# Decoder kernel on one core: the last stage regrouped into quads of heads on row and column tiles

## The reference, cut

```python
x = x + _L1_attn_ref(_layernorm(x), w_qkv, w_out, b_out)        # 16 heads of 32, key blocks of 128
x = x + _L1_xattn_ref(_layernorm(x), ctx, ctx, Wq, Wk, Wv, Wfc, bfc)  # 32 heads of 16, 8 key groups
x = x + _L1_ffn_ref(_layernorm(x), ...)   # base matmul + rank-16 adapters, gates top 2 of 6
# attention with blocks j of 128 keys:
m_ij = jnp.max(s, axis=-1, keepdims=True)
p = jnp.exp(s - m_ij)
l_ij = jnp.sum(p, axis=-1, keepdims=True)
m_new = jnp.maximum(m, m_ij)
alpha = jnp.exp(m - m_new)
beta = jnp.exp(m_ij - m_new)
l_new = alpha * l + beta * l_ij
out_new = alpha * l / l_new * out + beta * l_ij / l_new * pv
```

## Time and profile before

| | us |
|---|---|
| median of three runs | 3021.64 |
| lowest and highest | 2979.6, 3046.27 |
| profiled execution | 3025.3 |
| its span, first to last instruction | 3024.0 |
| PE busy | 2710.3 (90%) |
| DVE, ACT, POOL busy | 1141.2, 696.0, 569.6 |
| mean granted PE clock | 0.889 |

### The profile page before, as it was taken

One profiled execution on the slowest core, in us unless ns is written; L12 is line 12 of the kernel. 1 busy time (PEld: TensorE's weight loads), 2 busy tenths in 40 slices (PEclk: granted clock), 3 DMA queues, 4 the chain that ended last, 5 costly groups with the idle time before them and its releaser, 6 DMA issues.

```text
span 3024.0 us, 30202 instructions
## 1 busy us (share of the span) xinstructions
PE 2710.3 (90%) x10527; PEld 1605.8 (53%) x10527; DVE 1141.2 (38%) x2956; ACT 696.0 (23%) x2195; POOL 569.6 (19%) x1202
## 2 busy tenths in 40 slices
PE   7999999888699956999779999999998999999978
PEld 4555555555466633555446546464554645546544
DVE  2333433399522220111134534434354342534432
ACT  1111111000011101111133423424233251433412
POOL 0010110255100041111022221222112121221200
PEclk9777997699899987999969898988989899798979
DMA  4111110011222215222312002020020302103030
GB/s 150 35 35 35 63 35 21 25 42 44 106 80 87 80 35 174 63 63 63 99 58 44 23 10 56 15 58 22 22 44 15 58 22 44 37 1 59 1 58 8
DMA packets 93622, 150.62 MB, mean 50 GB/s; under 512 B 15472, under 2 KB 46960, under 8 KB 93344
## 3 DMA queue, kind: packets, MB, share of 16 engines
q1 hardware_dynamic: 86768, 130.05, 15.3%
q0 software_dynamic: 6704, 18.64, 2.2%
HBM read 106.33 MB, written 41.80 MB: 49 GB/s over the span
## 4 chain that ended last, share of the span: by engine, by line
PE 37%; issue 6%; DVE 3%; ACT 2%; POOL 2%; DMA 0%; DVEq 0%; SPq 0%; POOLq 0%; ACTq 0%
PE psum L1220 10%; PE psum L1341 8%; PE psum L1253 5%; PE psum L1309 3%; PE psum L1273 2%; PE psum L1262 2%; PE psum L1382 2%; PE psum L1330 2%; ACT probA L1435 1%; POOL yg L1679 1%; DVE xn L335 1%; DVE m_col L1629 1%; DVE statA L1580 1%; PE psum L346 1%; PE psum L1394 1%
## 5 line engine op out<-in xcount | busy, mean ns | idle before, releaser
L1341 PE MATMUL psum<-ex,va 128*32 128x256 f32 x1024 | 292.8, 415 | 24.4 <-ACT oe L1478 24.1
L1629 DVE TENSOR_REDUCE m_col<-psum 128x2 f32<-128x512 f32 x256 | 172.8, 686 | 123.6 <-PE psum L1309 123.6
L1435 ACT ACTIVATE probA<-psum,statA 128x128 f32<-128x128 f32 x512 | 180.8, 368 | 151.4 <-DVE statA L1580 151.4
L1472 ACT ACTIVATE ex<-psum 128x512 f32<-128x512 f32 x256 | 153.2, 602 | 197.1 <-PE psum L1330 194.5
L647 PE MATMUL psum<-kv,toep 128*128 128x288 f32 x640 | 165.2, 415 | 36.7 <-DVE z L663 32.4
L1047 PE MATMUL psum<-wgu,xgT 128*128 x624 | 190.2, 461 | 0.0
L442 PE MATMUL psum<-w,xnT 128*128 128x512 f32 x384 | 169.2, 598 | 6.8 <-DMA w<-in_wq 6.8
L1253 PE MATMUL psum<-kT,qT 32*128 32x256 f32 x512 | 169.0, 459 | 2.7 <-ACT statA L1439 2.7
L1341 PEld LDWEIGHTS psum<-ex,va 128*32 128x32 f32 x1024 | 97.1, 115 | 126.1 <-ACT oe L1478 28.9
L647 PEld LDWEIGHTS psum<-kv,toep 128*128 128x128 f32 x640 | 121.0, 193 | 80.7 <-issue 44.7
L1309 PE MATMUL psum<-k_stack,q_stack 48*128 48x256 f32 x512 | 144.4, 383 | 17.1 <-issue 13.4
(11 more groups left out here) (231 smaller groups left out, 4443.9 us busy)
## 6 DMA issues: line engine op xcount, KB each, us to landing
q_stack<-q_parts_d SPq DMA_DIRECT2D x48, 256.0 KB, 6.4
wgu<-in_exp_gate_up SPq DMA_DIRECT2D x8, 1408.0 KB, 7.5
ys_d<-ys SPq DMA_DIRECT2D x39, 256.0 KB
toep<-kpad_d SPq DMA_DIRECT2D x32, 256.0 KB, 3.0
q_parts_d<-q_part SPq DMA_DIRECT2D x32, 256.0 KB, 3.5
xin<-in_x SPq DMA_DIRECT2D x8, 512.0 KB, 5.7
cin<-in_ctx SPq DMA_DIRECT2D x8, 512.0 KB, 6.0
ctxT_d<-ctxT SPq DMA_DIRECT2D x8, 512.0 KB, 3.3
```

The costliest lines, as they stand in the source:

```text
L1341: i = pe.matmul(out_x[quad:quad + DA, 0:S], va[:, kt, h // 4, :], ex[n % 4][:, kt, :], start=kt == 0, stop=kt == TT - 1, skip_group_check= ...
L1435: act.activation(p[:, t, j * P:(j + 1) * P], src[:, (TT * t + j) * P:(TT * t + j + 1) * P], ACT.Exp, bias=s3[:, 0, TT * t + j:TT * t + j + 1],
L1472: act.activation(ex[n % 4][:, :, :].rearrange("p t s -> p (t s)"), ring_x.at[step, n], ACT.Exp).then_inc(s("x_exp"), 1)
L1629: dve.tensor_reduce(m_col[tile % 2][:, :, h % HPT], ring_x.at[step, n].rearrange("p (t k) -> p t k", t=TT), AX, ALU.max, negate=True).then ...
```

## The change

Heads go in quads. In self-attention a quad is one block m: four heads on the four groups of 32 partitions. `a_max` computes the scores of a quad with queries on the partitions (eight matmuls, four row tiles, four PSUM banks) only for the block maxima (two reduces of 1024 elements on DVE). `a_stat` makes the weights of the blocks, `a_rows` turns maxima and weights into rows, writes them to DRAM and reads them back: a row of negated maxima for each head (`mrow`) and the weights spread over 32 partitions each (`ab`). `a_exp` computes the scores again, transposed, and adds the maxima with a matmul of one contraction row; ACT takes the exponential in two pieces of 1024. `a_values` sums over the keys with a matmul against ones and multiplies with the values, both on four column tiles, and five DVE operations weight, add and divide. No transposes of probabilities, no scaling and no work on POOL are left there.

In cross-attention four key groups i stand 32 partitions apart (`q_spread`, `k_spread`), a quad is one query head c of each group. fp32r and the split into parts are gone: plain fp32 with 16 rows (17 with the maximum). `x_max`, `x_exp` and `x_values` work on quads (8 of each for a batch).

All eight banks are one ring for both threads (`Ring`), with takes of one bank or of an even pair. Of the order: x_k and x_v stand ahead of norm ln5, `base` stands behind `lowT`, norms, xb5 and xb6 have changed places, the routed rows are gathered in two halves through one buffer, and the totals of `together` are the threads' own sums.

```diff
+    def take(self, key, sem, n, wide=1):
+        k = self.n % self.size
+        if wide == 2 and k % 2:
+            k = (k + 1) % self.size
+        self.n = k + wide
+        before = self.freed[k:k + wide]
+        self.freed[k:k + wide] = [(sem, n)] * wide
+        self.at[key] = k
+        return k, before
...
+        return ([(0, 6000, "routed", b), (0, 1200, "routed_add", b, 0), (0, 6000, "routed_more", b),
+                 (0, 1200, "routed_add", b, 1)] + norm_steps("ln4", b) + [(0, 0, "xb4", b)] + turn_steps("x4", b))
...
+    def self_attention(b):
         out = []
...
+        for m in range(KD):
+            out += [(1710, 0, "a_qk", b, m, n) for n in range(2)] + [(860, 0, "a_max", b, m)]
+        out += [(0, 0, "a_stat", b)] + [(3430, 0, "a_v", b, t) for t in range(TT)] + [(220, 6500, "a_rows", b)]
+        quads = [("a_exp", 0), ("a_exp", 1), ("a_values", 0), ("a_exp", 2), ("a_values", 1), ("a_exp", 3), ("a_values", 2),
+                 ("a_values", 3)]
+        quads = [(1710, 0, step, b, m) for step, m in quads]
+        quads[-2:] = [quads[-2][:1] + (1500,) + quads[-2][2:], quads[-1][:1] + (3500,) + quads[-1][2:]]
+        out += side_by_side(quads, routed_in(b + 1) if b < B - 1 else [], 0)
+        return out + [(3430, 0, "a_out", b, t) for t in range(TT)]
...
+        quad = lambda step, a, c, wait=0: (860, wait, step, b, a, c)
+        out = [quad("x_max", 0, c) for c in range(4)] + [quad("x_max", 1, 0), (220, 0, "x_rows", b, 0)]
+        out += [quad("x_max", 1, c) for c in range(1, 4)]
+        out += [quad("x_exp", 0, 0), (220, 0, "x_rows", b, 1), quad("x_exp", 0, 1)]
+        every = [(a, c) for a in range(2) for c in range(4)]
+        for n in range(2, 8):
+            out += [quad("x_values", *every[n - 2]), quad("x_exp", *every[n])]
+            if n == 6:
+                out.append((880, 0, "x_divide", b, 0))
+        out += [quad("x_values", *every[6], 1000), (440, 0, "x_back", b, 0), quad("x_values", *every[7], 800)]
+        return out + [(880, 1800, "x_divide", b, 1), (440, 900, "x_back", b, 1)]
...
+        out = [(0, 0, "x_in", b), (1710, 0, "x_k", b), (1730, 0, "x_v", b)] + norm_steps("ln5", b) + [(0, 0, "xb5", b)]
+        out += turn_steps("x5", b)
+        out += [(1710, 4500 if m == KD - 1 else 0, "x_q", b, m) for m in range(KD)]
+        out += heads(b) + [(3430, 800 * t, "x_out", b, t) for t in range(TT)]
+        out += norm_steps("ln6", b) + [(0, 0, "xb6", b)] + turn_steps("x6", b)
+        out += [(820, 0, "low", b, t) for t in range(TT)]
+        out += [(0, 250, "gate", b, n) for n in range(3)] + [(0, 600, "gate", b, 3)]
+        out += [(0, 250, "gate", b, n) for n in range(4, 12)] + [(0, 600, "gated", b)]
+        return out + [(220, 0, "lowT", b)] + [(4290, 0, "base", b, t) for t in range(TT)] + [(0, 0, "out", b)]
 
...
+    ahead, behind = alone(self_attention(0)), alone(cross(0))
     for b in range(B - 1):
-        order += together((cross(b), 1.01 * ahead), (self_attention(b + 1), ahead))
+        order += together((cross(b), behind), (self_attention(b + 1), ahead))
...
+                    elif step == "a_rows":
+                        b, = a
+                        on_sp.wait_ge(s("a_row"), b + 1)
+                        on_sp.wait_ge(s("d_ab"), 80 * b)
+                        sp.dma_start(rows_d, mrows[:, :]).then_inc(s("d_rows"), 16)
+                        on_sp.wait_ge(s("d_rows"), 16 * (b + 1))
+                        on_sp.wait_ge(s("a_second"), KD * b)
+                        on_sp.wait_ge(s("a_w"), KD * b)
+                        by_head = rows_d.rearrange("(w m r j) s -> w r m j s", w=2, m=KD, r=HG)
+                        sp.dma_start(mrow[0:P:DA, :, :, :], by_head[0]).then_inc(s("d_ab"), 16)
+                        for r in range(HG):
+                            sp.dma_start(ab[DA * r:DA * r + DA, :, :], bass.AP(
+                                rows_d.tensor, (2 * HA + TT * r) * S, [[0, DA], [HG * TT * S, KD], [1, TT * S]])).then_inc(
+                                    s("d_ab"), 16)
...
+                    elif step == "a_max":
+                        b, m = a
+                        on_pe.wait_ge(s("qk1"), 8 * b + 2 * m + 2)
+                        two = [pe_take((step, b, m, p), s("a_m"), 8 * b + 2 * m + p + 1, 2) for p in range(2)]
                         for t in range(TT):
...
+                            for r in range(HG):
+                                c = slice(DA * r, DA * r + DA)
+                                i = pe.matmul(bank[two[r // 2] + r % 2][:, t * S:(t + 1) * S], qT1[c, m, part(t)], kT1[c, m, :],
+                                              start=True, stop=True)
...
+                        two = [pe_take((step, b, m, p), s("a_exp"), 8 * b + 2 * m + p + 1, 2) for p in range(2)]
                         for kt in range(TT):
...
+                            for r in range(HG):
+                                c = slice(DA * r, DA * r + DA)
+                                pe.matmul(bank[two[r // 2] + r % 2][:, kt * S:(kt + 1) * S], kT1[c, m, part(kt)], qT1[c, m, :],
+                                          start=True, stop=False)
...
+                        l = pe_take(("a_l", b, m), s("a_w"), n + 1)
+                        for j in range(TT):
+                            for r in range(HG):
+                                pe.matmul(bank[l][DA * r:DA * r + DA, j * S:(j + 1) * S], ones[:, 0:DA], e[:, r, j * S:(j + 1) * S],
+                                          start=True, stop=True, skip_group_check=True)
...
+                            for i in range(4):
+                                r = slice(DA * i, DA * i + DX)
+                                ins = pe.matmul(bank[two[i // 2] + i % 2][:, t * S:(t + 1) * S], q_spread[r, slot, part(t)],
+                                                k_spread[r, half, :], start=True, stop=True)
...
+                                r = slice(DA * i, DA * i + DX + 1)
+                                ins = pe.matmul(bank[two[i // 2] + i % 2][:, kt * S:(kt + 1) * S], k_spread[r, half, part(kt)],
+                                                q_spread[r, slot, :], start=True, stop=True)
...
+                            for i in range(4):
+                                ins = pe.matmul(bank[k][DA * i:DA * i + DA, 0:S], va[:, kt, 4 * half + i, :],
+                                                e[:, i, kt * S:(kt + 1) * S], start=kt == 0, stop=kt == TT - 1, skip_group_check=True)
...
+                        for p in range(2):
+                            k = ring.at[step, b, m, p]
+                            act.activation(e[:, 2 * p:2 * p + 2, :], psum[:, k:k + 2, :], ACT.Exp).then_inc(s("a_exp"), 1)
...
+                    elif step == "a_max":
+                        b, m = a
+                        on_dve.wait_ge(s("a_rT"), b)
+                        on_dve.wait_ge(s("a_first"), KD * b + m + 1)
+                        for p in range(2):
+                            k = ring.at[step, b, m, p]
+                            dve.tensor_reduce(mc[:, :, 0, m, 2 * p:2 * p + 2, :].rearrange("p t r j -> p r t j"),
+                                              psum[:, k:k + 2, :].rearrange("p r (t j k) -> p r t j k", t=TT, j=TT), AX, ALU.max,
+                                              negate=True).then_inc(s("a_m"), 1)
...
+                        b, m = a
+                        n = KD * b + m
+                        on_dve.wait_ge(s("d_ab"), 80 * (b + 1))
+                        on_dve.wait_ge(s("a_o"), n)
+                        on_dve.wait_ge(s("a_values"), n + 1)
+                        dve.tensor_tensor(wx[:, 0, :], bank[ring.at["a_l", b, m]], ab[:, m, :], ALU.mult).then_inc(s("a_w"), 1)
+                        on_dve.wait_ge(s("a_w"), n + 1)
+                        dve.tensor_tensor(wx[:, 1, :], bank[ring.at[step, b, m]], wx[:, 0, :], ALU.mult).then_inc(s("a_x"), 1)
+                        on_dve.wait_ge(s("a_x"), n + 1)
+                        dve.tensor_tensor(ds, wx[:, :, 0:S], wx[:, :, S:2 * S], ALU.add).then_inc(s("a_ds"), 1)
+                        on_dve.wait_ge(s("a_ds"), n + 1)
+                        dve.reciprocal(ds[:, 0, :], ds[:, 0, :]).then_inc(s("a_rc"), 1)
+                        on_dve.wait_ge(s("a_rc"), n + 1)
+                        on_dve.wait_ge(s("a_out"), 2 * b)
+                        dve.tensor_tensor(oT1[:, m, :], ds[:, 1, :], ds[:, 0, :], ALU.mult).then_inc(s("a_o"), 1)
...
+                        out = bank[pe_take((step, b, t), s("x6r"), 2 * b + t + 1)]
+                        for k in range(KD):
+                            pe.matmul(out, xT2[:, k, part(t)], load["w_base"][:, k, :], start=k == 0, stop=False)
                         on_pe.wait_ge(s("lowT"), b + 1)
```

633 lines of the change are left out of this document (258 added, 375 removed).

## The result

The changed kernel takes 2876.93 us (median of four runs, 2857.87 to 2883.43) against 3017.39 us on the same chip (four runs, 2979.6 to 3046.27): a ratio of 0.956, 95% interval 0.946 to 0.967. The forecast was 2833 us, range 2730 to 2950. Direction and size are right; the result lies 44 us above the point.

The account below looks back on a forecast made before the run. PE was taken to set the end. Work 103, waits 50 and clock 7 gave a period of 160 us against 178.6; saving 130, tail 44 and prologue 14 from 3024 gave 2836, as median 2833 us, range 2730 to 2950.

Parts of the forecast that it names:

- PE slots: PE work per period at full clock: 90.8 us removed, 42 added as quads, 61 unchanged; from 152 to 103, saving 49.
- The places of the waits: Where PE idles per period, including cT's load 2.7 us, a_exp for rows 4, turn of x6 11, gates 8.
- The reciprocal at its upper bound: DVE in a_values: reciprocal of 256 elements bounded by 0.42 and 1.78 us, the upper taken; 4.3 us a quad.
- The idle sum: PE's waits over one period, walked in the new order: 50 us in all, the largest 13 in x_max.
- The clock term: Per period: four idles, each followed by about 4 us of work at half clock, cost some 7 us.
- Tail: Cross part of the last batch alone: 105 us with half clock against 149 before, saving 44.
- with half clock 105: End of the tail's walk: 99 us, raised to 105 for work at half clock.
- rival 2: Clock stays at half over narrow work; over 3400 us with all 80 us on the path; chance 0.05 for slower.
- half clock over x_exp to x_out: A listed sign that the prediction is wrong: PE at half clock from x_exp through x_out.
- 1: Rival: only two tiles overlap, quads cost 1.73 us, period 186, total about 3040 us; chance 0.10.
- 3: Rival: waits are less than summed, period falls to 135 us, total about 2660; chance 0.08.
- 4: Rival: an unseen wait chain adds 10 us a period, 2906 total; slower only from +27, chance 0.02 for that.

Follow-up runs that it names:

- e8: Changed kernel with six unused full-width projections added in the tail only, one behind each of x_values 0 to 5 of the last batch; 2861.5 us (before 2988.42).
- e1: Changed kernel with all four matmuls of every score quad on one row tile, computing one head four times; 3865.88 us (before 3024.34).

## Why the prediction was right, and where its terms were off

- **PE slots: right.** 103 us of work after, 152 before, saved 49. Measured at the full clock in the steady periods: 108.5 and 152.9, saved 44. Counted by line (each record's own time multiplied by the granted clock), the quads come to 44.1 us against my 42 and the rest to 64.4 against my 61, so most of the 5.5 us is in the projections and turns, which I had taken from counts alone. The quads of x_exp cost 1.07 us and not 0.96; those of a_values 0.87.
- **The places of the waits: right but for one.** cT 2.2 (predicted 2.7), a_exp for the rows' DMA 6.7 (4, with bounds of 2 and 6, so just outside), the turn of x6 behind two a_values 10.1 (11), three short waits in a_max 1.4 for the 2.25 counted. In the place of the gates (8) PE waits 3.4, and in a steady period it is ln4's normalization that ends the wait. The reciprocal at its upper bound was right, 1.75 for 1.78.
- **The idle sum was mis-sized: 50 predicted, 32.4 measured.** The largest term, 13 us in x_max, is 4.9 us. DVE does bound that stretch as computed (reductions of 1.22, back to back), but PE's quads run there at half the clock, 2.09 us each, and so fill most of the gap. Their 6.1 us of clock and 4.9 of idle stand where I had 13 of idle. The gates were overcounted by 5 and a_exp's DMA undercounted by 3.
- **The clock term was mis-sized: 7 predicted, 22.9 measured.** I priced four starts behind an idle. Of the 16 us too many, eight quads at 2.09 for 1.15, 7.5 us, are six of x_max and the first two of x_exp, which wait for DVE and ACT in any case. The others are on the path: a_exp and a_values behind the wait for the rows, the turns, low and the first base. The errors cancel in the period (idle 18 less, clock 16 more, work 5.5 more), which is why 160 came so close to 163.8, and to the 161.0 of all seven. That is luck in part and no proof of the sum.
- **Tail: 105 predicted, 129 measured, of which 14 are not the tail's own.** My walk begins with x_k of the last batch. The stretch behind the last x4 addition begins earlier, with base of batch 6 (2752.4 to 2766.6 us, 3.9 of it a wait for the gates); the 149.3 us before, against which I set the 105, held such a piece too. In the periods the same 14 us are missing from the last one. From 2766.6 on the tail is 115.5 us, and nearly all of the difference to my 99 lies in one place. The windows' rows of the whole and of x_exp and x_values in it:

```profile
2766.60:2882.10 115.50, 87.20 (x539) 51.97 (x538) 32.51 (x59) 25.23 (x42) 6.38 (x6) 0.70 0.08 25
2809.59:2842.16 32.57, 31.50 (x270) 15.83 (x270) 3.36 (x5) 18.29 (x25) 0.00 (x0) 0.57 0.01 2
```

x_exp and x_values take 32.6 us and not 18: I had them bound by ACT, and at the 1.2 GHz level PE bounds them with 3.89 us a pair. Everything else together is 2 us above my walk. The mis-sized term is "with half clock 105", 6 us where 14.6 came. Rows 8 had shown the mechanism, narrow work with PE busy 18.36 of 20 us at 0.50, and I used it for rival 2 alone and not for the stretch where no full-width work is left. e8 shows this cause there. Of my own signs of being wrong, "half clock over x_exp to x_out" came true in this stretch for x_exp and x_values.
- **The 44 us by place.** Stages 1 to 4 took 10 us more in this execution, which is their own scatter; the prologue 6 more (118.8 for 113); the periods 21 more, when base of batch 6 is counted with them; the tail 10.5 more. That is 47, the span of 2882.1 less the 2836 of the sum being 46 by rounding; the medians are 44 apart.
- **Rivals.** 1 is excluded by e1 and by the quads of 1.07 us. 2 is real as a mechanism and small in this kernel: the clock costs 22.9 us in a period beside 17.9 before. In e1 it costs 88.1 us, and with what its extra work costs it makes the kernel 28% slower than before. 3 (smaller waits) is what the idle term showed, but the clock took it back. 4 does not show: the long waits of PE in a period are those that I had listed. The chances had a slip: slower 0.07 in all, but only 0.05 for it by the clock or a chain, beside 0.05 and 0.02 for these two.
